# A chunked gated-delta-rule layer with adaLN and experts: weighted k, token-major z, a select for the bound, and the identity product replaced by an addition

## The reference, cut to what matters

```
h = layernorm(x) * (1 + ca) + sa                      # x: 8 x 512 x 256
qkvz = h @ W_qkvz.T                                   # 16 k heads, 32 v heads of 128
q, k, v = silu(causal_conv4(qkv)); z is not convolved
beta = sigmoid(b); g = cumsum over a chunk of -exp(A_log) * softplus(a + dt_bias)
decay = where(tril, exp(g_i - g_j), 0)                # per chunk
A = -where(strict_tril, (k*beta) @ k.T * decay, 0)
T = inverse(I - A)
per chunk:  v_new = T @ (v*beta) - T @ (k*beta*exp(g)) @ state
            out   = (q*exp(g)) @ state + (q @ k.T * decay) @ v_new
            state = state * exp(g_last) + (k * exp(g_last - g)).T @ v_new
h = out * rsqrt(mean(out^2) + eps) * norm_weight * silu(z)
x = x + ga * (h @ W_out.T);  then a layernorm and 2 of 6 experts
```

## Time and profile before

| what | value |
|---|---|
| median of 3 runs (lowest, highest) | 4839.93 us (4837.36, 4840.07) |
| span of the profiled execution | 4831.3 us |
| PE busy, DVE busy, ACT busy, POOL busy | 97%, 91%, 72%, 57% |
| DMA | 24.7% of 16 engines, 78 GB/s |
| the attention's first and last projection record | 118 us, 4601 us |

### The profile page before, as it was taken

How to read it: one execution, slowest core, us unless ns; L and a number is a source line. 1 busy time by engine, 2 the same in 40 slices (tenths; PEclk the granted TensorE clock), 3 DMA queues, 4 the chain that set the end, 5 groups by cost and what they waited for, 6 DMA issues and landing times. The chain is left out here.

```text
span 4831.3 us, 132942 instructions
## 1 busy us (share of the span) xinstructions
PE 4671.0 (97%) x38533; PEld 3195.1 (66%) x38788; DVE 4411.5 (91%) x9152; ACT 3467.6 (72%) x8336; POOL 2743.0 (57%) x2329
## 2 busy tenths in 40 slices
PE   5899999999999999999999999999999999999978
PEld 3566666666666666666666666666666666666643
DVE  4899999999999999999999999999999999999953
ACT  3677777777777777777777777777777777777732
POOL 2456665656565665656566665656566665656520
PEclk7999999999999999999999999999999999999988
DMA  4222222222222222222222222222222222222122
GB/s 156 65 75 79 68 86 70 88 66 87 67 79 79 68 86 71 88 66 87 67 80 79 68 86 66 92 66 84 70 78 80 66 87 66 92 66 84 55 79 83
DMA packets 185165, 377.26 MB, mean 78 GB/s; under 512 B 86400, under 2 KB 95744, under 8 KB 184960
## 3 DMA queue, kind: packets, MB, share of 16 engines
q1 hardware_dynamic: 185088, 376.46, 24.7%
HBM read 360.13 MB, written 16.25 MB: 78 GB/s over the span
## 5 line engine op out<-in xcount | busy, mean ns | idle before, releaser
L658 PE MATMUL p_proj<-hid,w_in 128*128 128x512 f32 x3072 | 1626.7, 612 | 30.0 <-POOL ident_h L1185 28.9
L1018 DVE SCALAR_TENSOR_TENSOR conv<-p_proj,taps,conv 128x509 f32<-128x509 f32 (+2 forms) x1536 | 1134.8, 739 | 48.2 <-ACT conv L886 34.9
L1199 POOL TENSOR_TENSOR root<-sums,half_pow 128x8 f32<-128x8 f32 x128 | 210.8, 1647 | 862.9 <-DVE sums L1028 843.9
L1225 POOL TENSOR_SCALAR_AFFINE_SELECT x_bd<-x_t 128x512 bf16<-128x512 bf16 x640 | 422.6, 660 | 213.5 <-DVE x_t L1102 211.2
L658 PEld LDWEIGHTS p_proj<-hid,w_in 128*128 128x128 f32 x3072 | 497.3, 192 | 55.1 <-POOL ident_h L1185 29.1
L1093 DVE TENSOR_TENSOR y_h<-p_lev,y_h 128x512 bf16<-128x512 f32 x640 | 440.2, 688 | 74.4 <-PE p_lev L725 74.4
L868 PE MATMUL p_out<-h_t,w_out 128*128 128x512 f32 x1024 | 476.5, 608 | 2.2 <-DVE h_t L1164 1.1
L936 ACT ACTIVATE x_bd<-x_t 64x512 bf16<-64x512 bf16 x640 | 397.7, 621 | 96.3 <-DVE x_t L1102 96.2
L1102 DVE STREAM_TRANSPOSE x_t<-y_h 128x512 bf16<-128x512 bf16 x640 | 450.3, 704 | 4.5
L1072 DVE SCALAR_TENSOR_TENSOR ga<-p_out,neg_c,dec 128x256 f32<-128x256 f32 x1024 | 412.9, 477 | 35.4 <-ACT dec L924 34.8
L886 ACT ACTIVATE conv<-p_proj,taps 128x512 f32<-128x512 f32 x512 | 351.7, 687 | 121.9 <-PE p_proj L658 119.3
(11 more groups left out here) (213 smaller groups left out, 12562.4 us busy)
## 6 DMA issues: line engine op xcount, KB each, us to landing
w_in<-in_w_in SPq DMA_DIRECT2D x128, 768.0 KB, 6.3
g_row<-rows_scratch SPq DMA_DIRECT2D x128, 512.0 KB, 3.2
hid<-h_scratch SPq DMA_DIRECT2D x128, 512.0 KB, 7.4
e_row<-exp_rows_scratch SPq DMA_DIRECT2D x128, 512.0 KB, 5.3
w_out<-in_w_out SPq DMA_DIRECT2D x128, 256.5 KB, 2.7
x<-in_x SPq DMA_DIRECT2D x8, 512.0 KB, 10.6
h_scratch<-x SPq DMA_DIRECT2D x8, 512.0 KB, 2.6
y_scratch<-y_acc SPq DMA_DIRECT2D x8, 512.0 KB, 6.1
```

The source lines that it names most:

```text
L658: last = pe.matmul(p_proj[tile % 2][:], w_in[p][:, kt, tile * P:(tile + 1) * P], hid[p][:, kt, :], start=(kt == 0), stop=(kt == KT - 1))
L1018: dve.scalar_tensor_tensor(conv[:, tile, late:], p_proj[tile % 2][:, 0:S - late], taps[p][:, tile, j:j + 1], conv[:, tile, late:], ALU.mul ...
L1225: pool.affine_select(x_bd[:, :, HB:P], x_t[:], [[0, U], [0, HB]], ALU.is_ge, zero, base=-HB, channel_multiplier=1).then_inc(s["xbd_low"], 1)
```

## The change

It does six things, and the four order strings are written anew.

1. The weight of the state update goes to k: a new GpSimd task KW multiplies three chunks of `k_tok` by `w_c` for both v heads (one instruction, 128 x 768), VW is gone, and U becomes two 128-column matmuls per chunk that read `vx`.
2. z is projected token-major: the hidden state is the stationary operand, and P8 to P11 are two matmuls of 256 columns each. silu(z) is multiplied in on GpSimd, right behind the first multiplication of ON (a second instruction, 128 x 1024). HT only scales by the weight, and moves to ScalarE.
3. GL is an `affine_select` and no longer an addition; the constant triangle is gone.
4. W's product with the identity is gone; IV moves to VectorE and adds `x_dn` as it evicts.
5. p6 moves from VectorE to ScalarE as PH.
6. U waits for VX; D0 to KT and others get new lists of what held their PSUM bank last.

```diff
-PE_ORDER = ("M2@3 ON1@1 O0@2 VT0@3 Y2@3 KS1@2 W1@2 M3@3 TR1@2 P0@4 Y3@3 U1@2 P1@4 M4@3 KS2@2 O1@2 P2@4 Y4@3 TR2@2 "
+PE_ORDER = ("L@2 W0@1 G1@1 P11@2 TR0@1 M1@2 VT0@2 U0@1 Y1@2 O0@1 P0@3 M2@2 KS1@1 P1@3 Y2@2 TR1@1 W1@1 M3@2 U1@1 O1@1 ON0@0 "
...
-POOL_ORDER = ("SL@3 OP@1 XB1@3 ON@1 XB2@3 SD1@2 GL@4 XB3@3 QD@3 XB4@3 AR@3 SD2@2 AL@3 XB5@3 PW@4 RL@3")
+POOL_ORDER = ("RL@2 OP@1 SL@3 ON@1 XB1@3 SD1@2 XB2@3 AR@3 XB3@3 GL@5 SD2@2 XB4@3 AL@3 XB5@3 QD@3 KW@3 PW@4")
...
+                        for k in range(KT):
+                            last = pe.matmul(p_proj[tile % 2][:, kt * HD * DH:(kt + 1) * HD * DH],
+                                             hid[p][:, k, c * CH:(c + 1) * CH], w_in[p][:, k, 4 * P:6 * P],
+                                             start=(k == 0), stop=(k == KT - 1))
...
-                    pe.matmul(p_out[n][:], ident_h[:], quarter(x_dn, n).rearrange("p a i -> p (a i)"),
-                              start=True, stop=False)
...
-                    pe.matmul(p_a[:, HD * DH:2 * HD * DH], k_tok[p][:, n, :], vw[:].rearrange("p h f -> p (h f)"),
-                              start=True, stop=True).then_inc(s["u_mm"], 1)
+                    for h in range(HD):
+                        last = pe.matmul(p_a[:, (HD + h) * DH:(HD + h + 1) * DH], k_w[p][:, n, h, :], vx[:, h, :],
+                                         start=True, stop=True)
...
+                elif name == "PH":
...
+                    act.activation(p_h[HB:P], p_lev[HB:P, :].rearrange("p (u f) -> p u f", f=HB), ACT.Copy).then_inc(s["p6_done"], 1)
...
+                elif name == "HT":
...
+                    act.activation(cols(h_t, n), bank(n), ACT.Copy, scale=const["norm_w"]).then_inc(s["h_done"], 1)
...
+                elif name == "IV":
...
+                    dve.tensor_tensor(quarter(inv_t[p], n), bank(n), quarter(x_dn, n), ALU.add).then_inc(s["inv_done"], 1)
...
-                    pool.tensor_tensor(low[:], g_row[p][:], each(const["bound"], U), ALU.add).then_inc(s["g_low"], 1)
+                    pool.sem_inc(passed, 1)
+                    pool.affine_select(low[:], g_row[p][:], [[0, U], [1, CH]], ALU.is_ge, far_below, base=0,
+                                       channel_multiplier=-1).then_inc(s["g_low"], 1)
...
+                elif name == "KW":
+                    t.wait(pool, "k_tok_done")
+                    t.wait(pool, "w_scaled")
+                    t.wait(pool, "u_mm", back=2)
...
+                    t.wait(pool, "o_nrm", 1)
+                    t.wait(pool, "z_done")
+                    pool.tensor_tensor(o, o, z_t[p][:].rearrange("p c h f -> p (c h) f"), ALU.mult).then_inc(s["o_nrm"], 1)
```

More of the change, by code:

```diff
@@ L33 @@
 PAD = TAPS - 1
-PE_ORDER = ("M2@3 ON1@1 O0@2 VT0@3 Y2@3 KS1@2 W1@2 M3@3 TR1@2 P0@4 Y3@3 U1@2 P1@4 M4@3 KS2@2 O1@2 P2@4 Y4@3 TR2@2 "
[L35 to L40, removed]
[3 rows of a table removed]
-POOL_ORDER = ("SL@3 OP@1 XB1@3 ON@1 XB2@3 SD1@2 GL@4 XB3@3 QD@3 XB4@3 AR@3 SD2@2 AL@3 XB5@3 PW@4 RL@3")
+PE_ORDER = ("L@2 W0@1 G1@1 P11@2 TR0@1 M1@2 VT0@2 U0@1 Y1@2 O0@1 P0@3 M2@2 KS1@1 P1@3 Y2@2 TR1@1 W1@1 M3@2 U1@1 O1@1 ON0@0 "
+            "Y3@2 KS2@1 P2@3 M4@2 TR2@1 ON1@0 P3@3 U2@1 Y4@2 P4@3 KS3@1 VT1@2 M5@2 P5@3 O2@1 Y5@2 KT@3 P6@3 Q6@2 XD@2 QT@3 "
+            "TR3@1 P7@3 Z6@2 O3@1 D0@2 D1@2 P8@3 KK0@3 XC@2 KK1@3 P9@3 OY0@0 OY1@0 G0@2 P10@3")
+ACT_ORDER = ("AO@2 VK0@2 OT0@1 XB2@2 C0@3 VX1@1 Z1@2 XB3@2 OT1@1 OQ0@1 HT0@0 VX2@1 XB4@2 HT1@0 C1@3 OQ1@1 SK@3 XB5@2 VK1@2 C2@3 "
+             "SQ@3 KN@3 OT2@1 KT@3 PH@2 XD@2 VX3@1 QN@3 YC@2 C3@3 OQ2@1 OT3@1 OQ3@1 XC@2 SV0@3 GE@4 v0@2 SV1@3 VX0@2 XB1@3 Z0@3 "
+             "v1@2")
+DVE_ORDER = ("y2@2 X3@2 T0@3 q3@2 ST1@1 IV1@1 y3@2 RR2@1 X4@2 T1@3 q4@2 T2@3 ST2@1 y4@2 T3@3 X5@2 T4@3 q5@2 T5@3 SN2@2 y5@2 "
+             "SN0@2 s11@2 s10@2 RR3@1 KN@3 T6@3 T7@3 T8@3 QN@3 T9@3 F0@2 F1@2 SM0@3 SM1@3 SM2@3 SM3@3 OS0@1 GA0@3 GA1@3 OS1@1 "
+             "GA2@3 GA3@3 T10@3 YA0@0 T11@3 AB0@3 AB1@3 YA1@0 y0@3 IV0@2 X1@3 q1@3 ST0@2 SN1@3 y1@3 X2@3 q2@3 RR1@2")
+POOL_ORDER = ("RL@2 OP@1 SL@3 ON@1 XB1@3 SD1@2 XB2@3 AR@3 XB3@3 GL@5 SD2@2 XB4@3 AL@3 XB5@3 QD@3 KW@3 PW@4")
 def const_columns():
-    return [("ident", P), ("mean", P), ("ones", P), ("tri", P), ("bound", CH), ("eye", HB), ("mask", LEVELS * HB),
+    return [("ident", P), ("mean", P), ("ones", P), ("tri", P), ("eye", HB), ("mask", LEVELS * HB),
             ("upper", P), ("lower", P)]
@@ L426, in attention @@
         k_tok, v_tok = two("k_tok", [P, NC, DH]), two("v_tok", [P, NC, HD, DH])
+        k_w = two("k_w", [P, NC - 1, HD, DH])
         eye_h, ident_h = sb("eye_h", [P, HB], BF), sb("ident_h", [P, P], BF)
@@ L435, in attention @@
         state = two("state", [P, HD, DH])
-        rr, vx, vw = (sb(n, [P, HD, DH]) for n in ("rr", "vx", "vw"))
+        rr, vx = (sb(n, [P, HD, DH]) for n in ("rr", "vx"))
         state_dec = sb("state_dec", [P, HD, DH])
@@ L819, in emit @@
                 elif name == "U":
-                    t.wait(pe, "vw_done", n + 1)
+                    t.wait(pe, "vx_done", n + 1)
                     if n == 0:
-                        t.wait(pe, "k_tok_done")
+                        t.wait(pe, "kw_done")
                         t.wait(pe, "rr_done", back=1)
@@ L913, in emit @@
                     t.wait(act, "kt_mm")
-                    t.wait(act, "u_mm", back=2)
+                    t.wait(act, "kw_done", back=2)
                     act.activation(k_tok[p][:], bank(0), ACT.Copy).then_inc(s["k_tok_done"], 1)
@@ L939, in emit @@
                     t.wait(act, "w_mm", back=1)
+                    t.wait(act, "inv_done", back=1)
                     act.activation(x_dn[:].rearrange("p u i -> p (u i)"), p_tr_h, ACT.Copy).then_inc(s["xdn"], 1)
@@ L946, in emit @@
                        .then_inc(s["y21"], 1)
+                elif name == "PH":
+                    t.wait(act, "q6_mm")
+                    t.wait(act, "z6_mm", back=1)
+                    act.activation(p_h[HB:P], p_lev[HB:P, :].rearrange("p (u f) -> p u f", f=HB), ACT.Copy).then_inc(s["p6_done"], 1)
                 elif name == "XC":
@@ L986, in emit @@
                        .then_inc(s["ot_done"], 1)
+                elif name == "HT":
+                    t.wait(act, "on_mm", n + 1)
+                    t.wait(act, "y_out", back=1)
+                    act.activation(cols(h_t, n), bank(n), ACT.Copy, scale=const["norm_w"]).then_inc(s["h_done"], 1)
                 elif name == "OQ":
@@ L1051, in emit @@
                         t.wait(dve, "scaled")
+                        t.wait(dve, "kw_done", back=2)
                         dve.tensor_tensor(w_c[p][:], neg_c[p][:], w, ALU.mult).then_inc(s["w_scaled"], 1)
@@ L1154, in emit @@
                     t.wait(dve, "q_scaled", 1)
-                    t.wait(dve, "o_nrm", back=1)
+                    t.wait(dve, "o_nrm", 1, back=1)
                     dve.tensor_tensor(o_sc[:], o_ss[:], over(q_s2[p][:], [P, NC, HD]), ALU.mult).then_inc(s["osm"], 1)
```

123 lines of the change are left out of this document (54 added, 69 removed), and 3 rows, old and new, of the table DVE_ORDER.

## The result

The changed kernel takes 5709.03 us (5704.17 to 5719.75, 4 runs) against 4838.65 us in the same comparison: ratio 1.180, interval 1.179 to 1.182. The forecast of slower was right in sign and in the kind of wait; the sizes were not: the time lies above the stated range (4720 to 5600) and 549 us above the predicted 5160.

What follows compares the result with a forecast made beforehand. TensorE was taken to bound the pass, VectorE 1.6 us behind. Pass 34.4 us without collisions plus 3.2 for three collisions made 37.6, +2.5 on 35.09, +320 us over 128 passes: 5160, range 4720 to 5600.

Steps and rivals of the forecast that it cites:

- The forecast of slower: Whole kernel: slower than before, given 0.69, against faster 0.25 and same 0.06.
- Products: TensorE: identity products -0.43 us per pass, P8 to P11 nothing, U +0.03; sum -0.4.
- The identity product: TensorE, W: each takes 0.22 us, two go, so -0.43 us per pass.
- The pass without collisions: Rival: casts and small instructions get through or TensorE never waits for them; pass 34.4 us, 4750; chance 0.25.
- Loads: Work per pass: VectorE 31.4 us, ScalarE 0 to 0.7 on 26.4, GpSimd 23 to 24.
- First collision, SM behind F1: VectorE's SM2 is held by GpSimd's RL, which starts at F1's end, so OY0 waits for GA1; 1.3 us per pass.
- Second, AB behind SL: VectorE's casts AB are held by GpSimd's ON, L waits; 1.4 us, or 3.3 to 3.8 if the second multiplication slips between.
- Third, SN0 and s behind QD and KW: VectorE's SN0 and s are held by GpSimd's QD and KW ahead of XD; 0.5 us taken, 2.9 at most.
- The clock: TensorE's granted clock may leave 1.00 if it stands for microseconds; priced at nothing, to come on top.
- The sum: Three collisions of VectorE with GpSimd: 1.3 + 1.4 + 0.5 = 3.2 us per pass on 34.4.
- GpSimd gets the port whenever both wait: Rival: 3.6 us at AB and 2.9 at s, pass 42.2 us, 5750; chance 0.12.
- the products and KK: TensorE: 0.4 us of products and 0.3 of KK's standing go per pass, -90 us in all.

Runs made afterwards that it cites:

- split_z: `wait_os` with ON's second multiplication cut into two halves, XB1 between them, all work kept: 4778.08 us, ratio to before 0.988.
- no_z: `wait_os` with ON's second multiplication left out: 4747.39 us.
- wait_os: `wait_all`, only that RL waits for OS0 and not for the last SM instruction: 4875.18 us.
- wait_qd: Changed kernel, orders as they are, with one wait more: QD waits for s11 and s10: 5460.73 us.
- wait_on: Changed kernel, orders as they are, with one wait more: ON waits for the casts AB of the step two ahead: 5249.83 us.
- before_sm: Kernel before the change, with F1 moved ahead of the four SM instructions: 5145.15 us.
- ab_first: Changed kernel with the order around AB as before: SL ahead of OP, ON behind XB1, OS1 behind AB1: 5905.82 us.
- wait_all: Changed kernel, orders as they are, with three GpSimd waits: ON for casts AB, RL for SM, QD for s11 and s10: 4955.68 us, ratio to before 1.025.

## Why the prediction was right and where it failed

- Products. The identity product at 0.43 us per pass: 0.44 measured. The pass without collisions at 34.4: 34.6 with all work kept (`split_z`), 34.4 with one multiplication left out (`no_z`, 4747 us against the 4750 of that case). Both have waits that the changed kernel lacks; that kernel's own order without collisions is `wait_os`, 4875 (see the last point).
- Loads. In `split_z`, over 57.8 passes: VectorE 32.2 us, 0.8 more than predicted, ScalarE 27.2 (26.4 to 27.1), GpSimd 24.0 (23 to 24). In the changed kernel the select is 1.09 and KW 1.47, as priced; the second multiplication is 2.40, just above its bound of 2.36.
- First collision, SM behind F1: place and owner right, 1.3 predicted, a wait of 1.7 measured.
- Second, AB behind SL: place, owner and both cases were named, and the wrong one chosen. I took 1.4, both casts through between ON's two multiplications, and had 3.3 to 3.8 if the second slips in between the casts. It does: the casts take 4.25 us together, and L waits 3.1. This is the largest step that failed, +1.7 us. The second multiplication needs only a semaphore of the first, and the gap between them is 0.07 us (2062.28 to 2062.35), while two casts need 0.87; the second cast came at 2062.59 and found it running.
- Third, SN0 and s behind QD and KW: 0.5 predicted, 1.82 measured. The 0.5 was QD's part, and `w_c` is held for just that (698 ns against 156 in `wait_qd`). What failed is the argument that VectorE's own list puts s ahead of KW, which has to hear of SN0. That holds for the first copy (2045.35); KW asks at 2045.55 and is in before the second, which takes 1.49 us and not 0.29.
- The clock was priced at nothing, though named. By `wait_on` it costs 1.5 us per pass, all of it behind the longest wait; half of the 3.9 us per pass at the lower level would be 2.0 at the most.
- The sum: 1.7 + 3.1 + 1.8 = 6.6 where 3.2 stood, and 1.5 for the clock, on 34.4: 42.5 against about 42 measured. The result is nearest to the case "GpSimd gets the port whenever both wait" (5750), to which I gave 0.12; the range was cut off just below it. That nearness is in part luck: the case has 7.8 us of waits and nothing for the clock, and its rule is not what happened, for the first cast and the first copy got in ahead of a GpSimd instruction. Who asks first has it.
- In the kernel before, the covers were real: `before_sm` takes one away and pays 307 us. That the change gives back less than it should even without collisions (`wait_os` 4875) was a term that I left out: GpSimd's second multiplication stands ahead of XB1, 1.10 us per pass, and I had asked only what it does to AB. Through z_t it also fixes how late ON may come (`ab_first`).

What stays open: why 9 of the 48 waits for AB leave the clock at 2.4 GHz; and the casts on ScalarE in a good place, which was not tried.

## What to carry to other kernels

When an order is planned for VectorE and GpSimd side by side, write down for each VectorE instruction whether it reads SBUF alone by copy, cast or scalar, or has two SBUF inputs; each of these must find GpSimd idle or in an instruction that holds nobody, as the power here, or it pays the rest of GpSimd's instruction, however small it is itself. In a profile such a wait is booked as busy time of VectorE: look for one form whose mean is far above its shortest, and for another engine's record that ends with it. A single semaphore that holds GpSimd back for the length of the small instruction can be worth more than all the work that a change saves (here 459 us, where the products and KK were to save 90); and where several instructions of one kind stand in a row, count the gaps between them too.

## What the runs showed of the hardware

- GpSimd's power over 8 columns lasts 1.64 us and holds nobody, not even two-input instructions that start 0.17 us behind it. The Trainium skill (SBUF — State Buffer, Who interferes with whom) has such an instruction contend with every GpSimd one that reads SBUF; here the measurement decides, and it says no. Whether it holds the way in its first 0.17 us, and whether the operation or its mere 8 columns makes the difference, no run shows.
- VectorE's transposes in SBUF (702 ns) and its reciprocal (193) are not held by anything; scalar_tensor_tensor with two SBUF inputs is held as tensor_tensor is (2274 ns beside the multiplication).
- 0.03 us decide 1.7: in `wait_all` the same pair of instructions falls one way in one pass and the other way in the next, all through the run, so that the mean of the group (about half of the long value) shows neither.
- Behind a wait of 2.9 us TensorE ran 6 us of full work at 1.2 GHz (2065 to 2071). The same wait in other passes left 2.8 us at that level, or none; waits of up to 1.7 us in `wait_on` left none at all, and those of 2.0 to 2.2 in `before_sm` left some in 16 of 54 passes.
